# A two-layer cross-attention kernel on one core: plain fp32 scores on four row groups and normalisation by 32x32 block transposes

## The chip, the cores and the metric

One Trainium2 chip, one of its cores. The metric is the device time of one execution of the whole program in microseconds; less is better. Every input starts in HBM and the output ends there. TensorE (PE in the profile) multiplies, PEld is its weight load; DVE is VectorE, ACT is ScalarE, POOL is GpSimd, SP issues the transfers.

## The reference, cut to what matters

The inputs are `x` and `ctx`, each of shape (128, 128, 256): 128 independent tiles of 128 positions. All is fp32. Per tile:

```python
# layer 0: 16 heads of 16, rotary positions, feed-forward width 1024
h = ln(x, ln1);   q, k, v = h@sa_wq, h@sa_wk, h@sa_wv        # plus biases, q scaled, q and k rotated
x = x + softmax(q k^T, causal) v @ sa_wo + sa_bo
h = ln(x, ln2);   q = h@ca_wq;   k, v = ctx@ca_wk, ctx@ca_wv  # plus biases, rotated
x = x + softmax(q k^T) v @ ca_wo + ca_bo
h = ln(x, ln3);   x = x + gelu(h@fc1_w + fc1_b)@fc2_w + fc2_b
# layer 1: fuse, one head of width 256, keys = values = ctx
t = softmax(x ctx^T) ctx
out = tanh([x, t] @ trans_W + trans_b) + x
```

## The kernel before

**Precision.** Most products are done in three fp32r passes, as hi*hi + hi*lo + lo*hi (`split3`, L337 to L342), for which each operand is split: ScalarE or VectorE copies the hi part from PSUM, VectorE subtracts for the lo part (`sub`, L626). PV (L481) and one fuse product (L575) are plain fp32; the trace records each plain fp32 matmul as two.

**The pipeline.** Every engine runs the same hand-written slot (`slot(i, u)`), one new tile per slot, four slots in a loop body. In a slot four tiles are in flight: `a` (first layer norm, self q/k/v, first self scores), `k` = a-1 (second self scores, exponentials, PV, cross keys and values), `m` = a-2 (self output, layer norm 2, the whole cross-attention, layer norm 3) and `f` = a-4 (second feed-forward product and fuse). Every second slot ends in f1, the first feed-forward product for two tiles, followed by gelu (ScalarE), hid_hi (GpSimd) and hid_lo (VectorE). The order of work on each engine is the order in which its `slot` calls the steps; semaphores join the engines, and there is no scheduler. PSUM has eight banks: four are the scores `sc`, and A0, A1, B0, C0 are shared by all the rest.

**Softmax of one chain** (`c` is "s" for self, "c" for cross). The maximum over keys must be known per query before the exponential, but the exponential is taken on transposed scores (keys on partitions), so scores are computed twice:

- q and its low part are put side by side (`qs_hi`, `qs_lo`), k is doubled (`twice`: `kd`, `kcd`), so that one head fills 32 rows, hi and lo. TensorE transposes them (`trq`, `trk`, `trkc`), and ScalarE writes q as a block-diagonal `qt` in four copies of 32 rows (L921, 4 x 577 ns), keys as `skt_hi`/`kct_hi` with VectorE's `skt_lo`/`kct_lo`.
- `scores` (L442): 16 fp32r matmuls of 128x128 with all 128 rows; the self chain first adds a bf16 mask (L424). Each group of four signals.
- `maxima` (L757): four VectorE reductions of 128x512, as each group arrives. `trm` (L455) transposes the 16 maxima, `mdiag` (L762) spreads them.
- `scores_t` (L465, L470): four K=32 matmuls add the negative maximum, eight 128x512 matmuls add the scores. Each pair signals, and `exps` (L947) follows group by group; then `pv` (L481), whose ones columns give the softmax sums.
- Normalisation: ScalarE copies PV out (`osb`), TensorE transposes (`tro`), VectorE takes a reciprocal (L769) and multiplies (L771), TensorE transposes back (`tra`), `at_hi` and `at_lo` split, and `y` multiplies in six fp32r passes. `residual` (L791) adds x and starts the next layer norm, in whose wait for the GpSimd power the cross chain does one self maximum (`meanwhile`).

```python
if X: scores("c", m)      # TensorE, before, around the cross scores
if A: trk(a)
if F: fs(f)
if X: trm("c", m)
if A: trq("s", a)
if X: scores_t("c", m)
if F: trfa(f)
if X: pv("c", m)
if F: fy(f)
```

Of the kernel before, what the change touches and what calls it, by code (L numbers as in the profile page):

```python
# [44 lines left out]
def build(nc, d, out_d):  # L45
    ctx = ExitStack()
    with ctx:
# [48 lines left out]
        kct_hi = sb("kct_hi", [P, G, P], F32R)  # L96
        kct_lo = sb("kct_lo", [P, G, P], F32R)
        skt_hi = sb("skt_hi", [P, G, P], F32R)
        skt_lo = sb("skt_lo", [P, G, P], F32R)
# [27 lines left out]
        qs = {c: sb(f"qs_{c}", [P, H, 2, HD], F32R) for c in "sc"}  # L127

        qt = dict.fromkeys("sc", sb("qt", [P, G, G, P], F32R))
        nm = {c: sb(f"nm_{c}", [P, G, 32], F32R) for c in "sc"}  # L130
        mdiag = dict.fromkeys("sc", sb("mdiag", [P, G, P], F32R))
# [5 lines left out]
        osb = {c: sb(f"osb_{c}", [P, G, P]) for c in "sc"}  # L137
        rinv = {c: sb(f"rinv_{c}", [P, H]) for c in "sc"}
        att = dict.fromkeys("sc", sb("att", [P, H, HD]))
        at_hi = dict.fromkeys("sc", sb("at_hi", [P, KC, P], F32R))  # L140
        at_lo = dict.fromkeys("sc", sb("at_lo", [P, KC, P], F32R))
        mask_f, mask_tf = osb["s"][:, 0, :], osb["s"][:, 1, :]
# [28 lines left out]
        per_chain = ("qs_hi", "qs_lo", "trq", "qt", "sc", "nm", "trm", "mdiag", "sct", "exp", "pv", "osb", "tro",  # L171
                     "rinv", "att", "tra", "at_hi", "at_lo", "y", "x", "xres")
# [959 lines left out]
```

## Time and profile before

| | us |
|---|---|
| median of 3 runs | 5721.84 |
| lowest, highest | 5720.23, 5731.34 |
| span of the profiled execution (first to last instruction) | 5720.3 |
| TensorE busy, 34992 matmuls | 4624.6 |
| TensorE weight loads busy | 3728.5 |
| VectorE busy, 7863 instructions | 3590.9 |
| ScalarE busy, 5121 instructions | 2441.3 |
| GpSimd busy, 1924 instructions | 1298.8 |
| mean granted TensorE clock | 0.920 of full |

The profiled execution's own time is not listed apart from the three runs; its span lies 1.5 us under their median and within their spread. How to read it: an engine's busy time is the sum over all its instructions, so it doesn't tell who waits for whom. A granted clock of 1.00 is 2.4 GHz, 0.50 is 1.2 GHz. A matmul's duration in a row contains its latency; what it costs the queue is the distance of the starts.

### The profile page before, as it was taken

The page shows a single profiled execution, that of the slowest core. Times are in us where ns is not written, and L with a number is a line of the kernel's source. Part 1 is how long each engine was busy: PE and PEld are TensorE (multiplying, and loading weights), DVE is VectorE, ACT ScalarE, POOL GpSimd, SP SyncE. Part 2 cuts the span into 40 slices and gives each one's busy share as a digit, 9 for nine tenths or more (in the row PEclk, how much of TensorE's full clock was granted, in tenths as well). Part 3 has the DMA queues.
Part 4 walks back from the last instruction along what each step waited for, and adds up shares of the span by engine and source line. Part 5 has one row for each costly group of instructions (what it writes and reads, how often), then busy time and mean ns, then how long its engine had stood idle before and what let it go on. Part 6 is the DMA issues. An engine that isn't in the chain of part 4 may idle for free.

```text
span 5720.3 us, 99465 instructions
## 1 busy us (share of the span) xinstructions
PE 4624.6 (81%) x34992; PEld 3728.5 (65%) x34992; DVE 3590.9 (63%) x7863; ACT 2441.3 (43%) x5121; POOL 1298.8 (23%) x1924
## 2 busy tenths in 40 slices
PE   4888888888888888888888888888888888888886
PEld 3666666666666666666666666666666666666665
DVE  4666666666666666666666666666666666666663
ACT  1444444444444444444444444444444444444442
POOL 0222222222222222222222222222222222222221
PEclk7899999999999999999999999999999999999997
DMA  1000000000000000000000000000000000000000
GB/s 55 9 10 10 9 12 10 10 10 12 9 10 12 10 10 10 11 10 10 10 12 9 10 12 10 10 12 10 10 10 12 10 9 11 11 10 10 12 6 5
DMA packets 64812, 63.61 MB, mean 11 GB/s; under 512 B 9648, under 2 KB 64048, under 8 KB 64304
## 3 DMA queue, kind: packets, MB, share of 16 engines
q1 hardware_dynamic: 64304, 56.61, 3.2%
q8 instruction: 346, 5.67, 0.4%
q14 instruction: 162, 1.33, 0.1%
HBM read 39.81 MB, written 16.78 MB: 10 GB/s over the span
## 4 chain that ended last, share of the span: by engine, by line
PE 48%; DVE 25%; issue 16%; POOL 6%; ACT 3%; DVEq 0%; POOLq 0%; ACTq 0%
PE sc L470 10%; DVE nm_c L757 5%; PE B L335 4%; PE A L340 3%; PE A L342 3%; PE A L341 3%; POOL hid_hi L1076 3%; PE C L340 3%; PE C L342 3%; PE C L341 3%; PE B L340 2%; PE A L481 2%; PE sc L465 2%; PE B L481 2%; DVE at_lo L626 2%
## 5 line engine op out<-in xcount | busy, mean ns | idle before, releaser
L947 ACT ACTIVATE pt<-sc 128x512 f32<-128x512 f32 x1024 | 564.1, 599 | 415.0 <-PE sc L470 402.8
L1046 POOL TENSOR_TENSOR rstd<-bmv,eps_t 128x1 f32<-128x1 f32 x384 | 72.7, 189 | 1894.9 <-DVE bmv L674 1894.9
L626 DVE TENSOR_TENSOR hid_lo<-hid,hid_hi 128x512 fp32r<-128x512 f32 x256 | 264.7, 1070 | 353.2 <-POOL hid_hi L1076 353.2
L921 ACT CAST qt<-B 32x512 fp32r<-32x512 f32 x512 | 295.7, 577 | 183.9 <-PE B L335 179.4
L1076 POOL TENSOR_TENSOR hid_hi<-hid,ones_f 128x512 fp32r<-128x512 f32 x256 | 264.7, 1054 | 453.4 <-ACT hid L977 452.7
L757 DVE TENSOR_REDUCE nm_s<-sc 128x4 fp32r<-128x512 f32 x512 | 338.8, 682 | 12.4 <-PE sc L442 5.7
L335 PE MATMUL B<-ident,att 128*128 128x128 f32 x512 | 114.9, 308 | 279.3 <-DVE att L771 279.3
L757 DVE TENSOR_REDUCE nm_c<-sc 128x4 fp32r<-128x512 f32 x512 | 316.2, 674 | 0.0
L340 PE MATMUL C<-w_f_hi,hid_hi 128*128 128x256 f32 x1024 | 302.4, 295 | 3.6 <-POOL hid_hi L1076 3.0
L678 DVE TENSOR_SCALAR xhat<-x,bmv,rstd 128x256 f32<-128x256 f32 x256 | 207.0, 808 | 144.3 <-POOL rstd L1048 144.3
L921 ACT CAST qt<-A 32x512 fp32r<-32x512 f32 x512 | 294.9, 576 | 4.7 <-PE A L335 0.3
L470 PE MATMUL sc<-qt,kct_hi 128*128 128x512 f32 x512 | 294.5, 575 | 0.0
L335 PEld LDWEIGHTS B<-ident,att 128*128 128x128 f32 x512 | 59.2, 147 | 360.1 <-DVE att L771 346.8
L342 PE MATMUL C<-w_f_hi,hid_lo 128*128 128x256 f32 x1024 | 289.3, 282 | 0.0
L341 PE MATMUL C<-w_f_lo,hid_hi 128*128 128x256 f32 x1024 | 289.0, 282 | 0.0
L1082 POOL TENSOR_TENSOR o_out<-fpre,x 128x256 f32<-128x256 f32 x128 | 93.2, 728 | 829.9 <-ACT fpre L995 829.9
L442 PE MATMUL sc<-skt_hi,qt 128*128 128x128 f32 x2048 | 270.7, 286 | 0.0
L887 ACT CAST h3t_hi<-B 128x256 fp32r<-128x256 f32 x128 | 47.6, 372 | 521.2 <-PE B L335 521.2
L470 PE MATMUL sc<-qt,kct_lo 128*128 128x512 f32 x512 | 267.1, 522 | 0.0
L442 PEld LDWEIGHTS sc<-skt_hi,qt 128*128 128x128 f32 x2048 | 252.4, 194 | 19.1 <-issue 0.8
L470 PE MATMUL sc<-qt,skt_hi 128*128 128x512 f32 x512 | 263.2, 514 | 0.0
L442 PEld LDWEIGHTS sc<-kct_hi,qt 128*128 128x128 f32 x2048 | 248.0, 191 | 13.5 <-ACT qt L921 2.7
(249 smaller groups left out, 14323.5 us busy)
## 6 DMA issues: line engine op xcount, KB each, us to landing
rows_in<-in_x SPq DMA_DIRECT2D x128, 128.0 KB, 2.0
rows_in<-in_ctx SPq DMA_DIRECT2D x128, 128.0 KB, 2.1
out<-o_out SPq DMA_DIRECT2D x128, 128.0 KB, 1.7
pt<-in_L_xattn_fc_w SPq DMA_DIRECT2D x1, 1024.0 KB, 4.8
rows_in<-in_L_xattn_fc_w SPq DMA_DIRECT2D x1, 1024.0 KB, 6.8
pt<-in_L_xattn_sa_wq SPq DMA_DIRECT2D x1, 256.0 KB, 8.6
rows_in<-in_L_xattn_sa_wk SPq DMA_DIRECT2D x1, 256.0 KB, 8.6
pt<-in_L_xattn_sa_wv SPq DMA_DIRECT2D x1, 256.0 KB, 2.7
```

The costliest lines, as they stand in the source:

```text
L335: t = pe.transpose(out[:, k * P:(k + 1) * P], src[:, k * P:(k + 1) * P], ident[:, :])
L340: pe.matmul(out, a_hi, b_hi, start=first, stop=False, skip_group_check=True)
L341: pe.matmul(out, a_hi, b_lo, start=False, stop=False, skip_group_check=True)
L342: return pe.matmul(out, a_lo, b_hi, start=False, stop=last, skip_group_check=True)
L442: mm = pe.matmul(sc[:, g, b * P:(b + 1) * P], qt[c][:, g, b, :], kh[:, g, :], start=(b == 0 and c == "c"), stop=(b == G - 1), skip_group_c ...
L470: mm = pe.matmul(sc[:, g, :], kk[:, g, :], qt[c][:, g, :, :].rearrange("p b q -> p (b q)"), start=False, stop=(kk is kl), skip_group_check ...
L481: mm = pe.matmul(bank_of[c]["pv"][32 * b:32 * b + 32, g * P:(g + 1) * P], vaug[c][at[1] % 2][:, G * g + b, :], pt[c][:, g, b, :], start=Tr ...
L626: dve.tensor_tensor(out, a, hi.bitcast(F32), ALU.subtract).then_inc(signal, 1)
L757: dve.tensor_reduce(nm[c][:, g, 0:G], sc[:, g, :].rearrange("p (b k) -> p b k", b=G), AX_X, ALU.max, negate=True).then_inc(sc_[c]["nm"], 1)
L921: w = act.copy(qt[c][part, :, b, :], bank_of[c]["q"][part, :].rearrange("p (g q) -> p g q", q=P))
L947: act.activation(pt[c][:, g, :, :].rearrange("p b q -> p (b q)"), sc[:, g, :], ACT.Exp)\
L1076: pool.tensor_tensor(hid_hi[:, 2 * c:2 * c + 2, :], hid[c % 2][:, :, :], ones_f[:, :].unsqueeze(1).broadcast_to([P, 2, M * P]), ALU.mult). ...
```

## The change

Two parts, in both attention chains.

**Scores.** q and k are no longer split. `rope` writes them with a stride of 32 columns per head into `qkz`, `qcz`, `kcz`: 16 features, a 17th and 15 zeros. After a transpose (plain, the same 4 x 128x128) one head lies in one 32-row group of `qt`/`kt`, copied by ScalarE in one 128x512 copy. `scores` uses the 16 feature rows of each head: 16 plain fp32 matmuls, the four row groups in turn, each group writing its own bank. `maxima` writes the negative maximum straight into the 17th column of q (whose partner in k is one), in two reductions of 128x1024 after all 16 matmuls; `trqm` transposes q again (four transposes), `qtm_` copies it, and `scores_t` is 16 plain fp32 matmuls with all 32 rows. `exps` waits for all of them.

**Normalisation.** VectorE transposes the 32x32 blocks of PV's bank (`ot_`, L722), takes the reciprocal, multiplies in two halves, and transposes the blocks again into `at_t` (L737); `y` is two plain fp32 matmuls against output weights whose rows are loaded in a permuted order (`w_out`, eight small transfers). `ot_("s", k)` stands on VectorE after the cross rope of the same slot, `ot_("c", m)` after `fpre`. osb, tro, tra, at_hi and at_lo are gone.

```diff
@@ TensorE
-                for g in range(G):
-                    for b in range(G):
-                        mm = pe.matmul(sc[:, g, b * P:(b + 1) * P], qt[c][:, g, b, :], kh[:, g, :],
-                                       start=(b == 0 and c == "c"), stop=(b == G - 1), skip_group_check=True)
-                    mm.then_inc(sc_[c]["sc"], 1)
+                    for r in range(G):
+                        rows = slice(32 * r, 32 * r + HD)
+                        mm = pe.matmul(sc[:, r, g * P:(g + 1) * P], qt[c][rows, g, :], kt[c][rows, g, :],
+                                       start=(g == 0 and c == "c"), stop=(g == G - 1), skip_group_check=True)
+                mm.then_inc(sc_[c]["sc"], 1)
...
-                pe.transpose(bank_of[c]["m"][:, 0:P], nm[c][:, :, :].rearrange("p b g -> p (b g)").bitcast(F32),
-                             ident[:, :]).then_inc(sc_[c]["trm"], 1)
+                transposes(bank_of[c]["m"], qz[c].rearrange("p h e -> p (h e)"), G).then_inc(sc_[c]["trqm"], 1)
...
+                pe.wait_ge(sc_[c]["qtm"], n(at))
                 for g in range(G):
-                    pe.matmul(sc[:, g, :], ones_r[32 * g:32 * g + 32, :],
-                              mdiag[c][32 * g:32 * g + 32, :, :].rearrange("p b q -> p (b q)"), start=(c == "c"),
-                              stop=False, skip_group_check=True)
-                for g in range(G):
-                    for kk in (kh, kl):
-                        mm = pe.matmul(sc[:, g, :], kk[:, g, :], qt[c][:, g, :, :].rearrange("p b q -> p (b q)"),
-                                       start=False, stop=(kk is kl), skip_group_check=True)
-                    mm.then_inc(sc_[c]["sct"], 1)
+                    for r in range(G):
+                        rows = slice(32 * r, 32 * r + 32)
+                        mm = pe.matmul(sc[:, r, g * P:(g + 1) * P], kt[c][rows, g, :], qt[c][rows, g, :],
+                                       start=(g == 0 and c == "c"), stop=(g == G - 1), skip_group_check=True)
+                mm.then_inc(sc_[c]["sct"], 1)
...
-                    mm = split3(bank_of[c]["y"][:, 0:E], at_hi[c][:, k, :], at_lo[c][:, k, :], w_hi[w][:, k, :],
-                                w_lo[w][:, k, :], k, k == 0, k == KC - 1)
+                    mm = pe.matmul(bank_of[c]["y"][:, 0:E], at_t[c][:, k, :], w_out[c][:, k, :], start=(k == 0),
+                                   stop=(k == KC - 1))
@@ VectorE
-            def maxima(c, at, groups):
-                for g in groups:
-                    dve.wait_ge(sc_[c]["sc"], G * n(at, 0) + g + 1)
-                    dve.tensor_reduce(nm[c][:, g, 0:G], sc[:, g, :].rearrange("p (b k) -> p b k", b=G),
+            def maxima(c, at, halves):
+                dve.wait_ge(sc_[c]["sc"], n(at))
+                for h in halves:
+                    out = qz[c].rearrange("p (g r) e -> p r g e", r=G)[:, 2 * h:2 * h + 2, :, HD]
+                    dve.tensor_reduce(out, sc[:, 2 * h:2 * h + 2, :].rearrange("p r (g k) -> p r g k", g=G),
                                       AX_X, ALU.max, negate=True).then_inc(sc_[c]["nm"], 1)
...
+            def ot_(c, at):
+                dve.wait_ge(sc_[c]["pv"], n(at))
+                dve.transpose(ot[c][:, :, :, :].rearrange("p r b j -> p (r b j)"), bank_of[c]["pv"][:, :])\
+                    .then_inc(sc_[c]["ot"], 1)
...
+                for k in range(KC):
+                    w = dve.tensor_tensor(att[c][:, k, :, :, :].rearrange("p b s e -> p s b e"),
+                                          ot[c][:, 2 * k:2 * k + 2, :, 0:HD],
...
+                dve.transpose(at_t[c][:, :, :].rearrange("p k q -> p (k q)"),
+                              att[c][:, :, :, :, :].rearrange("p k b s e -> p (k b s e)")).then_inc(sc_[c]["at_t"], 1)
@@ VectorE, slot
-                if X: qs_lo("c", m)
+                if K: ot_("s", k)
...
-                if A: qs_lo("s", a)
-                if X: maxima("c", m, range(G))
-                if A: skt_lo_(a)
-                if X: mdiag_("c", m)
+                if X: maxima("c", m, (0, 1))
...
+                if X: ot_("c", m)
                 if X: normalise("c", m)
-                if X: at_hi_("c", m)
-                if X: at_lo_("c", m)
-                if K: kct_lo_(k)
                 if X: residual("c", m, a if A else None)
+                if X: h3t_lo_(m)
                 if A: maxima("s", a, (1,) if X else (0, 1))
-                if X: h3t_lo_(m)
-                if A: maxima("s", a, (2, 3))
```

On TensorE, from the cross scores of a tile to its output projection. `kd`, `qs_s`, `kcd` are the doubled or split q and k, `nm_c` the maxima. Before:

```order
L442 MATMUL sc<-kct_hi,qt 128x128 x16
L335 MATMUL A<-ident,kd 128x128 x4
L455 MATMUL B<-ident,nm_c 128x128
L335 MATMUL A<-ident,qs_s 128x128 x4
L465 MATMUL sc<-mdiag,ones_r 128x512 x4
L470 MATMUL sc<-qt,kct_hi 128x512
L470 MATMUL sc<-qt,kct_lo 128x512
```

and the changed kernel, where `qkz` and `qcz` are the widened q and k:

```order
L433 MATMUL sc<-kt_c,qt_c 128x128 x16
L333 MATMUL A<-ident,qkz 128x128 x4
L333 MATMUL B<-ident,qcz 128x128 x4
L333 MATMUL A<-ident,qkz 128x128 x4
L454 MATMUL sc<-qt_c,kt_c 128x128 x16
L465 MATMUL B<-pt,vaug_c 32x128 x16
L333 MATMUL A<-ident,kcz 128x128 x4
L478 MATMUL B<-w_out_c,at_t_c 128x256 x2
```

The second score block is 16 matmuls of 128 columns in place of four and eight of 512, one maximum transpose became four, and the transposes between PV and the projection went.

On VectorE, from fpre to the reciprocal of the next slot. Before:

```order
L837 TENSOR_TENSOR fpre<-C,bias_t 128x256
L769 RECIPROCAL rinv_c<-B 128x16
L771 TENSOR_TENSOR att<-B,rinv_c 128x256
L777 CAST at_hi<-B 128x256
L626 TENSOR_TENSOR at_lo<-B,at_hi 128x256
L626 TENSOR_TENSOR kct_lo<-A,kct_hi 128x512
L791 TENSOR_TENSOR x<-B,xres_c 128x256
```

and the changed kernel:

```order
L792 TENSOR_TENSOR fpre<-C,bias_t 128x256
L722 STREAM_TRANSPOSE ot_c<-B 128x512
L727 RECIPROCAL rinv_c<-ot_c 128x16
L730 TENSOR_TENSOR att_c<-ot_c,rinv_c 128x2x4x16 x2
L737 STREAM_TRANSPOSE at_t_c<-att_c 128x256
L746 TENSOR_TENSOR x<-B,xres_c 128x256
L640 BN_STATS bst<-x 128x6
L642 COPY dtick<-eps_t 128x1
L643 BN_AGGR bmv<-bst 128x2
L717 TENSOR_REDUCE qkz<-sc 128x2x4
L647 TENSOR_SCALAR xhat<-x,bmv,rstd 128x256
```

Two block transposes took the place of the two splits, and the self maximum ahead of xhat now covers two banks.

## Rows read from the trace of the kernel before

**Rows 1.** The page: busy time of each engine; the chain that ended last.
```profile
PE 4624.6 (81%) x34992; PEld 3728.5 (65%) x34992; DVE 3590.9 (63%) x7863; ACT 2441.3 (43%) x5121; POOL 1298.8 (23%) x1924
...
PE 48%; DVE 25%; issue 16%; POOL 6%; ACT 3%; DVEq 0%; POOLq 0%; ACTq 0%
```

**Rows 2.** Timeline, VectorE: start us, us, engine line op, out<-in, xcount [idle before].
```profile
2825.51 0.26 DVE L769 RECIPROCAL rinv_s<-B 128x16 f32<-128x16 f32 x1 [1.83 <-issue]
...
2829.79 0.42 DVE L791 TENSOR_TENSOR x<-B,xres_s 128x256 f32<-128x256 f32 x1 [1.29 <-PE B L342]
...
2858.83 0.42 DVE L791 TENSOR_TENSOR x<-B,xres_c 128x256 f32<-128x256 f32 x1
...
2864.30 0.25 DVE L769 RECIPROCAL rinv_s<-B 128x16 f32<-128x16 f32 x1
...
2867.89 0.42 DVE L791 TENSOR_TENSOR x<-B,xres_s 128x256 f32<-128x256 f32 x1 [0.52 <-issue]
...
2896.76 0.42 DVE L791 TENSOR_TENSOR x<-B,xres_c 128x256 f32<-128x256 f32 x1 [0.17 <-PE B L342]
...
2911.81 0.24 DVE L769 RECIPROCAL rinv_s<-B 128x16 f32<-128x16 f32 x1
```

**Rows 3.** Timeline, TensorE: cross scores and fuse product of both slots, first f1.
```profile
2843.05 1.90 PE L442 MATMUL sc<-kct_hi,qt 128*128 128x128 f32 x16
...
2853.65 0.70 PE L575 MATMUL C<-cw,fatt_t 128*128 128x256 f32 x2
...
2881.03 1.90 PE L442 MATMUL sc<-kct_hi,qt 128*128 128x128 f32 x16
...
2891.56 0.70 PE L575 MATMUL C<-cw,fatt_t 128*128 128x256 f32 x2
...
2901.12 0.36 PE L340 MATMUL A<-h3t_hi,w_f_hi 128*128 128x256 f32 x1 [0.97 <-DVE h3t_lo L626]
```

**Rows 4.** Windows of 1 us, TensorE: length, busy (matmuls), granted clock, DMA, GB/s.
```profile
2830.00:2831.00 1.00, 1.00 (x6) 0.50 0.00 0
...
2850.00:2851.00 1.00, 1.00 (x4) 0.50 0.00 0
...
2864.00:2865.00 1.00, 0.56 (x3) 1.00 0.00 0
```

**Rows 5.** Timeline, TensorE: self scores, mask, four transposes.
```profile
2859.26 2.09 PE L442 MATMUL sc<-skt_hi,qt 128*128 128x128 f32 x16
...
2864.60 1.03 PE L424 MATMUL sc<-mask_t_bf,ident_bf 128*128 128x512 bf16 x4
...
2885.58 0.63 PE L335 MATMUL A<-ident,qs_s 128*128 128x128 f32 x4
```

**Rows 6.** Timeline, TensorE, windows to 2873.65, 2873.75 and around 2867.9.
```profile
2873.58 0.32 PE L481 MATMUL A<-pt,vaug_s 128*32 128x128 f32 x4 [0.16 <-DVE tqk L717]
...
2873.58 0.43 PE L481 MATMUL A<-pt,vaug_s 128*32 128x128 f32 x8 [0.16 <-DVE tqk L717]
...
2867.73 0.51 PE L465 MATMUL sc<-mdiag,ones_r 32*128 32x512 f32 x4
```

**Rows 7.** Timeline, VectorE (qs_lo, fpre, the normalised x) and ScalarE (exponentials).
```profile
2882.24 0.51 DVE L626 TENSOR_TENSOR qs_s<-qkf,qs_s 128x256 fp32r<-128x256 f32 x1
...
2893.01 0.42 DVE L837 TENSOR_TENSOR fpre<-C,bias_t 128x256 f32<-128x256 f32 x1 [2.65 <-PE C L342]
...
2860.93 0.81 DVE L678 TENSOR_SCALAR xhat<-x,bmv,rstd 128x256 f32<-128x256 f32 x1 [0.18 <-POOL rstd L1048]
...
2868.95 2.07 ACT L947 ACTIVATE pt<-sc 128x512 f32<-128x512 f32 x4 [2.69 <-PE sc L470]
```

**Rows 8.** Groups of instructions by form: busy us, mean ns | idle before.
```profile
L757 DVE TENSOR_REDUCE nm_c<-sc 128x4 fp32r<-128x512 f32 x512 | 316.2, 674 | 0.0
...
L762 DVE TENSOR_TENSOR mdiag<-B,dmask 128x512 fp32r<-128x512 f32 x128 | 86.2, 673 | 1.0 <-PE B L455 1.0
...
L887 ACT COPY osb_c<-B 128x512 f32<-128x512 f32 x128 | 75.0, 586 | 53.3 <-PE B L481 53.3
```

More of the change, by code:

```diff
@@ L95, in build @@
                 "c": [sb(f"vaug_c{i}", [P, H, 2 * HD]) for i in range(2)]}
[L96 to L99, printed above, removed]
+        kt = {c: sb(f"kt_{c}", [P, G, P]) for c in "sc"}
         tqk = sb("tqk", [P, 2 * E])
@@ L125, in build @@
         o_out = [sb(f"o_out{i}", [P, E]) for i in range(2)]
[L127 to L131, printed above, removed]
+        qt = {c: sb(f"qt_{c}", [P, G, P]) for c in "sc"}
         pt = dict.fromkeys("sc", sb("pt", [P, G, G, P]))
@@ L136, in build @@
         ln_brep = x2b_all[:, 0:3 * KC * P].rearrange("p (l k n) -> p l k n", l=3, k=KC)
-        osb = {c: sb(f"osb_{c}", [P, G, P]) for c in "sc"}
+        ot = {c: sb(f"ot_{c}", [P, G, G, 2 * HD]) for c in "sc"}
         rinv = {c: sb(f"rinv_{c}", [P, H]) for c in "sc"}
[L139 to L142, printed above, removed]
+        att = {c: sb(f"att_{c}", [P, KC, G, 2, HD]) for c in "sc"}
+        at_t = {c: sb(f"at_t_{c}", [P, KC, P]) for c in "sc"}
+        mask_f, mask_tf = [at_t["s"][:, k, :] for k in range(2)]
         xres = {"s": [sb(f"xres_s{i}", [P, E]) for i in range(2)], "c": [sb("xres_c", [P, E])] * 2}
@@ L170, in build @@
         s = {n: sem("s_" + n) for n in names}
-        per_chain = ("qs_hi", "qs_lo", "trq", "qt", "sc", "nm", "trm", "mdiag", "sct", "exp", "pv", "osb", "tro",
-                     "rinv", "att", "tra", "at_hi", "at_lo", "y", "x", "xres")
+        per_chain = ("trq", "qt", "sc", "nm", "trqm", "qtm", "sct", "exp", "pv", "ot",
+                     "rinv", "att", "at_t", "y", "x", "xres")
         sc_ = {c: {n: sem(f"s_{c}_{n}") for n in per_chain} for c in "sc"}
@@ L396, in trq @@
             def trq(c, at):
-                pe.wait_ge(sc_[c]["qs_hi"], n(at))
-                pe.wait_ge(sc_[c]["qs_lo"], n(at))
+                pe.wait_ge(s["qkf" if c == "s" else "qcf"], n(at))
                 if c == "s":
@@ L531, in f1 @@
                 need(pe, s["fpre"], n(f))
-                for q in ("kct_hi", "kct_lo", "tkc", "v_c"):
+                for q in ("kct", "tkc", "v_c"):
                     pe.wait_ge(s[q], n(k))
-                for q in ("skt_hi", "skt_lo"):
-                    pe.wait_ge(s[q], n(a))
+                pe.wait_ge(s["skt"], n(a))
                 for c in range(FC):
```

223 lines of the change are left out of this document (81 added, 142 removed).

## The prediction

> **What bounds the kernel now.** I read the page first: TensorE is busy for 81% of the span and VectorE for 63%, yet the chain that ended last lies on TensorE for only 48% of its length, on VectorE for 25%, and 16% is issue [rows 1]. So no engine is the bound alone. The program is a loop of hand-ordered slots in which TensorE, ScalarE, VectorE and GpSimd pass one tile on to each other, and a saving counts only where one of them waits for it.
>
> So I cut one pair of slots (two tiles) into stages, by the VectorE timeline and the TensorE timeline. Slot A runs from the reciprocal at 2825.51 to the one at 2864.30, slot B, which ends in the first feed-forward product, to 2911.81: 86.30 us for the pair [rows 2]. 64 pairs make 5523 us, the rest of the 5720.3 us span is setup, fill and drain. The stages, A then B [rows 2, 3]:
> - 1, self-attention's normalisation and output projection, reciprocal to x: 4.28 and 3.59.
> - 2, x to the first cross scores: 13.26 and 13.14.
> - 3, cross scores, maximum, second scores, exponentials, PV, to the fuse product L575: 10.60 and 10.53.
> - 4, L575 to cross-attention's x: 5.18 and 5.20.
> - 5, x to the next reciprocal in A, 5.47; to the first f1 product in B, 4.36.
> - 6, only in B: f1, gelu, the hid_hi/hid_lo chain, to the reciprocal, 10.69.
>
> The third view is the granted clock. It stands at 0.50 (1.2 GHz) in A's stage 1 and in stage 3, and at 1.00 around the start of B's stage 1 [rows 4]. In each half-rate stretch TensorE had done little but transposes before.
>
> **The score blocks.** Scores were 16 fp32r matmuls, 2.09 us in the self case [rows 5]; now they are 16 fp32 matmuls of 128 columns on four 32-row groups. The trace has both halves of that. The plain fp32 PV product (four column groups) starts four passes together: x4 last 0.32, x8 last 0.43, so 0.107 us per four passes [rows 6]. Four K=32 matmuls of 512 columns on four row groups last 0.51 together [rows 6], little more than one alone would. 32 passes in eight bursts give 7 x 0.107 + 0.28 = 1.03 us to the last result. Bounds: 1.0, if row groups behave as column groups do; 16 x 0.107 + 0.2 = 1.9, if the two passes of a matmul run one behind the other; 32 x 0.107 = 3.4, if nothing overlaps. I take 1.03, by the nearest row, and use it in both directions of the scores. The Trainium skill, TensorE: Matmul & The Clock Gate, "What overlaps and what doesn't", says matmuls start and end strictly in program order. By that rule the block would be 1.9; the PV rows speak against it, so it stays a rival.
>
> **Stage 3, both slots.** S is the first cross score. VectorE's qs_lo goes, which took 0.51 from S+1.21 [rows 7], just ahead of the maxima; they now start at S+1.25, after the block's end at S+1.06. Four reductions of 674 ns [rows 8] step by 0.60; two of twice the size step by 1.13 and end at S+3.6. Then four transposes, 0.63 [rows 5], in place of one; a copy of 0.59 by ScalarE (its row: 586 ns [rows 8]) in place of mdiag's 0.67 [rows 8]; the block, at S+4.95 instead of S+6.2. Its exponentials now wait for the whole block (S+6.15) and take 2.07 [rows 7] to 2.2, so S+8.3; PV's last quarter adds 0.25. L575 starts at S+8.55, 2.0 earlier than the mean of 10.56. That is at full clock. At half, block, PV tail and L575's products cost 1.85 more. The quiet stretch before the block begins earlier and ends earlier than today's, so I charge half of that: -1.08 per slot.
>
> **Stage 4, both slots.** After L575, fpre (1.45 later, 0.44 with its hand-over [rows 3, 7]) still comes first on VectorE. Then the 512-wide block transpose, which no row shows: I take 0.69, a little over the 512-wide mdiag of 673 ns [rows 8]; the reciprocal 0.29; two half-size multiplies, 0.5; a 256-wide transpose, 0.42, like the 256-wide x [rows 2]. TensorE's two rounds of transposes, osb, at_hi and at_lo go. The plain fp32 projection has four passes of 256 columns; two such in L575 last 0.70 [rows 3], so four last 1.13 against 0.75. Sum 5.03, -0.17. The bounds of the wide transpose: 0.67 (the mdiag and reduction rows), and twice 0.69, since nothing here excludes half rate.
>
> **Stage 5.** The mask (four matmuls, 0.68 before the next starts) is unchanged, scores end at x+1.5, and the first maximum now needs all of them: x+1.55 instead of x+1.2, and lasts 1.13 instead of 0.6. The normalisation waits for it, at x+2.72 instead of x+2.10, but then runs beside no GpSimd work (0.42, like x [rows 2], instead of 0.81 [rows 7]). Sum: +0.15 in A, +0.2 in B.
>
> **Stage 1.** In A, at half clock: reciprocal, multiplies, transpose 1.2, projection 1.95, x at 3.3: -1.0. In B, TensorE first has four transposes where one was and then the mask, so the projection starts at 1.4 and x comes at 2.5 at full clock, 4.6 at half. Between scores (end 2861.35) and mask (2864.60) there are 3.25 us without matmuls today, at 1.00 [rows 4, 5]; that stretch grows to 4.6, nearer to the long ones that end at 0.50. I take 4.0: +0.4.
>
> **Stages 2 and 6.** Stage 2's products and their VectorE queue are untouched; qs_hi, twice and the four-part qt copies (ScalarE), and qs_lo, skt_lo, kct_lo (VectorE) go, all beside TensorE's f2 to kvc products, so nothing is gained; the moved 0.69 us transpose of the self chain is hidden there too, and would cost its own 0.69 if those products were shorter. Exponentials that start later push x2t_hi back: +0.2 and +0.25. f1 may begin at half clock after the longer quiet: +0.3 for stage 6. Setup loses two weight splits and gains eight transfers, within 3 us, at nothing.
>
> Sum: A -1.0 +0.2 -1.08 -0.17 +0.15 = -1.90; B +0.4 +0.25 -1.08 -0.17 +0.2 +0.3 = -0.10. That is -2.0 us per pair, -128 us, a span of 5592 from 5720.3. The shown median, 5721.84, stands 1.5 above that span, so 5594.
>
> **The rivals.**
> - The clock. TensorE sheds over a tenth of its work, and each quiet stretch is longer. If the half-rate stretches also cover the mask and scores of stage 5 (+1.7 each) and all of stage 3 (+0.92 each), the pair is +5.2, +335 us: 5930; half of that, which I find likelier, is 5760. It decides from +2.0 us per pair on, that is, when one of the two stage 5s and one stage 3 run at 1.2 GHz. For it: the rows at 0.50 today. Against: the long dense run of stage 2 lifts the clock each time. Chance 0.2.
> - Passes in order: +0.75 (maxima late), +0.85 (second block), +0.85 (stage 5), +0.15 elsewhere, 2.6 per slot, 5.2 per pair: 5927. For it the page's rule, against it the PV rows. Chance 0.12.
> - Block transposes at half rate: +1.1 in stage 4, +0.4 in stage 1 per slot, 3.0 per pair: 5786. Chance 0.06.
> - The clock stays up: stage 3 at full (-1.85 per pair), B's stage 1 at 2.5 (-1.5), stages 2 and 6 without their charges (-0.6): -3.95, -253 us: 5341. Against: rows 4. Chance 0.1.
> - Gains and losses cancel (the change surely does what it says: the order rows show the new queues). Within 0.2%, about what a measurement of this kernel can tell from no change: 5710 to 5733. Chance 0.05.
>
> **How the numbers follow.** The forecast, 5594, has what is left, 0.47, and spans about 5500 to 5700. Faster: forecast 0.47, clock up 0.1, and a tenth or two of the clock rival's low end: 0.61. Same 0.06. Slower 0.33. The range must hold eight in ten: it reaches down over half of the clock-up case to 5440 and up over the half-rate transposes and most of the clock rival to 5860; passes in order stays outside.
>
> **What would show it.** Each score block in the new trace: 1.0 us at full clock, eight starts of four passes 0.107 apart (1.9 would mean passes in order). The 512-wide transpose near 0.69. The pair near 84.3 us; stage 3 near 9.5 and near 8.6 where the clock is 1.00; stage 5 slightly longer. Mean granted clock a little under 0.92; under 0.85 the clock rival holds. The forecast is wrong if stage 3 isn't a microsecond shorter, or if stage 5 or 1 grows by more than that.

## The result, and the profile after

The changed kernel takes 5982.66 us (median of 4, 5971.28 to 6004.51) against 5721.53 us: ratio 1.0454, 95% interval 1.0437 to 1.0472. It is slower by 261 us; 5594 us was forecast, and the range ended at 5860. The profiled execution spans 5969.5 us with a mean granted clock of 0.846, where the kernel before spans 5720.3 us at 0.920.

The page, beside [rows 1]: busy time of the engines, the granted clock in 40 slices, the chain that ended last.

```profile
PE 4462.0 (75%) x42928; PEld 3482.7 (58%) x42928; DVE 3205.1 (54%) x6966; ACT 1706.6 (29%) x3713; POOL 1330.2 (22%) x1924
...
PEclk9888888888888888888898888888888888888887
...
issue 43%; PE 20%; DVE 18%; POOL 11%; ACT 6%; DMA 0%; SPq 0%; POOLq 0%; DVEq 0%; ACTq 0%
```

Every engine but GpSimd does less work, as intended: VectorE 386 us less, ScalarE 735 us less, TensorE 163 us less. TensorE's saving is that small because much of what is left runs at half rate: in experiment x4, where the clock is higher, TensorE is busy for 4403 us, 479 of them with added idle matmuls. The kernel is longer all the same, so the time went into waits and into slower work. "issue", which grew from 16% to 43% of the chain, does not tell slow from fast here: it reads 44% in x4 and 41% in x12, the fastest kernel below.

The VectorE timeline over a pair of slots, beside [rows 2]:

```profile
2846.34 0.24 DVE L727 RECIPROCAL rinv_s<-ot_s 128x16 f32<-128x16 f32 x1
...
2849.46 0.42 DVE L746 TENSOR_TENSOR x<-B,xres_s 128x256 f32<-128x256 f32 x1 [1.23 <-issue]
...
2878.46 0.42 DVE L746 TENSOR_TENSOR x<-B,xres_c 128x256 f32<-128x256 f32 x1 [1.28 <-PE B L478]
...
2884.43 0.24 DVE L727 RECIPROCAL rinv_s<-ot_s 128x16 f32<-128x16 f32 x1
...
2889.19 0.42 DVE L746 TENSOR_TENSOR x<-B,xres_s 128x256 f32<-128x256 f32 x1 [2.87 <-issue]
...
2919.01 0.42 DVE L746 TENSOR_TENSOR x<-B,xres_c 128x256 f32<-128x256 f32 x1 [2.22 <-PE B L478]
...
2936.36 0.25 DVE L727 RECIPROCAL rinv_s<-ot_s 128x16 f32<-128x16 f32 x1
```

The TensorE timeline of the same pair, beside [rows 3, 5]:

```profile
2864.10 1.17 PE L433 MATMUL sc<-kt_c,qt_c 16*128 16x128 f32 x32
2869.09 1.17 PE L454 MATMUL sc<-qt_c,kt_c 32*128 32x128 f32 x32 [0.24 <-ACT qt_c L836]
...
2877.24 1.13 PE L478 MATMUL B<-w_out_c,at_t_c 128*128 128x256 f32 x4 [2.53 <-DVE at_t_c L737]
2878.20 1.03 PE L415 MATMUL sc<-mask_bf,ident_bf 128*128 128x512 bf16 x4
...
2912.47 0.70 PE L547 MATMUL C<-cw,fatt_t 128*128 128x256 f32 x2
...
2916.84 2.08 PE L478 MATMUL B<-w_out_c,at_t_c 128*128 128x256 f32 x4 [2.53 <-DVE at_t_c L737]
2918.71 1.60 PE L415 MATMUL sc<-mask_bf,ident_bf 128*128 128x512 bf16 x4
2920.24 1.17 PE L433 MATMUL sc<-kt_s,qt_s 16*128 16x128 f32 x32
```

The score blocks last 1.17 us (1.03 forecast). The same projection lasts 1.13 us in slot A and 2.08 in slot B, and both times TensorE had sat idle for 2.53 us before it. The granted clock in 1 us windows of slot B, beside [rows 4], shows why:

```profile
2915.00:2916.00 1.00, 0.00 (x0) 1.00 0.00 0
2916.00:2917.00 1.00, 0.15 (x1) 0.72 0.00 0
2917.00:2918.00 1.00, 1.00 (x3) 0.50 0.38 131
...
2920.00:2921.00 1.00, 1.00 (x26) 1.00 0.00 0
...
2922.00:2923.00 1.00, 0.00 (x0) 1.00 0.00 0
2923.00:2924.00 1.00, 0.55 (x2) 0.64 0.00 0
...
2929.00:2930.00 1.00, 1.00 (x6) 0.50 0.07 16
2930.00:2931.00 1.00, 1.00 (x10) 0.95 0.00 0
```

TensorE idles at 1.00 while VectorE normalises, the clock drops to 0.50 (1.2 GHz) just as projection and mask begin, is back at 1.00 (2.4 GHz) for the scores, idles through the layernorm and drops again for the first 5 us of f1. What stands behind the quiet stretch pays for it, on the path. The same stage of this one trace says it without any comparison of kernels. Here is B4 in three pairs that follow each other (columns as in [rows 4]):

```profile
2734.83:2741.37 6.54, 4.02 (x21) 0.81 0.14 46
2823.92:2829.52 5.60, 3.08 (x22) 1.00 0.08 26
2912.47:2919.01 6.54, 4.01 (x21) 0.80 0.12 42
```

The stage lasts 5.60 us at a clock of 1.00 and 6.54 at 0.8.

The new VectorE work, by form (busy us, mean ns | idle before). The transposes are means of like instructions; the 546 ns of att_c are not, see x7:

```profile
L730 DVE TENSOR_TENSOR att_c<-ot_c,rinv_c 128x128 f32<-128x128 f32 x256 | 129.3, 546 | 4.4
...
L722 DVE STREAM_TRANSPOSE ot_c<-B 128x512 f32<-128x512 f32 x128 | 90.3, 706 | 6.7 <-PE B L465 6.7
...
L737 DVE STREAM_TRANSPOSE at_t_c<-att_c 128x256 f32<-128x256 f32 x128 | 57.0, 445 | 4.4
```

One pair is a sample, since the clock falls in other places in the next. So here are the stages as means in us over some 55 pairs of each trace, cut by the same rows (first and last start of each stage); the forecast's own charge stands beside them, and the last column is experiment x4, below.

| stage | before | forecast | after | after − before | x4 − before |
|---|---|---|---|---|---|
| A1 | 4.00 | −1.0 | 3.34 | −0.66 | −1.12 |
| A2 | 13.83 | +0.2 | 14.68 | +0.85 | +0.79 |
| A3 | 10.27 | −1.08 | 9.13 | −1.14 | −1.51 |
| A4 | 5.19 | −0.17 | 6.29 | +1.10 | +0.41 |
| A5 | 5.46 | +0.15 | 6.58 | +1.12 | +0.51 |
| B1 | 3.62 | +0.4 | 4.71 | +1.09 | −0.92 |
| B2 | 13.10 | +0.25 | 14.14 | +1.04 | +1.07 |
| B3 | 10.38 | −1.08 | 8.86 | −1.52 | −1.62 |
| B4 | 5.20 | −0.17 | 6.16 | +0.96 | +0.40 |
| B5 | 4.36 | +0.2 | 5.59 | +1.23 | +0.59 |
| B6 | 11.67 | +0.3 | 11.82 | +0.15 | −0.98 |
| pair | 87.08 | −2.0 | 91.31 | +4.23 | −2.37 |

What was to get faster did. What was charged at next to nothing, the stages that hold projection, mask and self scores, grew by more than a microsecond each. 64 pairs of +4.23 make +271 us, the whole difference of the spans (249) and a little more.

One row of the table, B6, hides two effects. In the kernel before it alternates (a loop body holds two pairs), and not by the clock: in experiment x6, below, both lengths stand at 1.00.

```profile
2812.92:2825.51 12.59, 8.05 (x61) 0.98 0.01 3
2901.12:2911.81 10.69, 8.06 (x61) 1.00 0.01 2
```

In the longer one VectorE stands idle for 1.83 us ahead of the reciprocal and waits for nothing that the profile shows [rows 2]. The pair that the forecast was read from ends in the short one. The changed kernel doesn't have this: in x4, at a clock of 1.00, B6 is 10.69 us in every pair. So the change wins 1 us per pair there that nobody forecast, and the clock takes it back (11.82 against 10.69). What causes the wait no run shows; x1, with the new scores alone, hasn't got it, and x2 has.

### The profile page after: what moved, and what is told of

It is laid out like the page before. It is cut to its first block, busy times and chain, and to the rows that moved or that the text cites. A ratio compares the mean times of both kernels' runs of the same rounds, so it can differ in the third digit from the quotient of the medians.

```text
span 5969.5 us, 110993 instructions
## 1 busy us (share of the span) xinstructions
PE 4462.0 (75%) x42928; PEld 3482.7 (58%) x42928; DVE 3205.1 (54%) x6966; ACT 1706.6 (29%) x3713; POOL 1330.2 (22%) x1924
## 4 chain that ended last, share of the span: by engine, by line
issue 43%; PE 20%; DVE 18%; POOL 11%; ACT 6%; DMA 0%; SPq 0%; POOLq 0%; DVEq 0%; ACTq 0%
PE B L478 4%; POOL hid_hi L996 4%; ACT pt L882 4%; PE sc L454 3%; POOL qkf L957 3%; DVE qkz L717 3%; DVE qcz L717 3%; PE B L333 2%; PE sc L415 2%; DVE att_c L730 2%; PE A L333 2%; POOL kcf L957 2%; POOL xres_c L981 2%; PE sc L433 2%; DVE ot_c L722 1%
## 5 line engine op out<-in xcount | busy, mean ns | idle before, releaser
L836 ACT COPY qt_c<-B 128x512 f32<-128x512 f32 x256 | 150.3, 587 | 1140.2 <-PE B L333 1140.2
L478 PE MATMUL B<-w_out_c,at_t_c 128*128 128x256 f32 x512 | 224.2, 583 | 320.4 <-DVE at_t_c L737 320.4
L717 DVE TENSOR_REDUCE qkz<-sc 128x8 f32<-128x1024 f32 x256 | 312.4, 1221 | 170.2 <-PE sc L433 170.2
L333 PE MATMUL A<-ident,qkz 128*128 128x128 f32 x1536 | 283.0, 315 | 99.8 <-DVE qkz L717 89.2
L478 PE MATMUL B<-w_out_s,at_t_s 128*128 128x256 f32 x512 | 231.0, 600 | 154.4 <-DVE at_t_s L737 154.4
L717 DVE TENSOR_REDUCE qcz<-sc 128x8 f32<-128x1024 f32 x256 | 301.6, 1221 | 7.2 <-PE sc L433 1.3
L333 PE MATMUL B<-ident,qcz 128*128 128x128 f32 x1024 | 165.0, 284 | 168.4 <-DVE qcz L717 164.6
L465 PE MATMUL B<-pt,vaug_c 128*32 128x128 f32 x4096 | 217.0, 291 | 91.2 <-ACT pt L882 73.8
L478 PEld LDWEIGHTS B<-w_out_s,at_t_s 128*128 128x128 f32 x512 | 148.0, 302 | 229.6 <-issue 192.2
L333 PEld LDWEIGHTS A<-ident,qkz 128*128 128x128 f32 x1536 | 196.7, 159 | 144.0 <-DVE qkz L717 114.0
```

The source lines that it names most:

```text
L333: t = pe.transpose(out[:, k * P:(k + 1) * P], src[:, k * P:(k + 1) * P], ident[:, :])
L465: mm = pe.matmul(bank_of[c]["pv"][32 * g:32 * g + 32, r * P:(r + 1) * P], vaug[c][at[1] % 2][:, G * g + r, :], pt[c][:, r, g, :], start=Tr ...
L478: mm = pe.matmul(bank_of[c]["y"][:, 0:E], at_t[c][:, k, :], w_out[c][:, k, :], start=(k == 0), stop=(k == KC - 1))
L717: dve.tensor_reduce(out, sc[:, 2 * h:2 * h + 2, :].rearrange("p r (g k) -> p r g k", g=G), AX_X, ALU.max, negate=True).then_inc(sc_[c]["nm ...
L836: act.copy(out, src).then_inc(signal, 1)
```

## The experiments

The theory: TensorE lost work between its bursts, the quiet stretches end at 1.2 GHz more often, and the work behind them pays. Its first rival: VectorE's chain is longer and collides with GpSimd, and TensorE only waits for it. Its second: one of the two parts of the change alone is the loss. Times below are medians against runs of the kernel before on the same chip.

**x1 and x2: the parts apart.** x1 keeps the old normalisation (osb, two rounds of transposes, hi/lo split, fp32r projection) and has the new scores; x2 keeps the old scores and has the new normalisation, with w_out's rows permuted to the old order of heads. The main edit of each, x1 against the changed kernel and x2 against the one before:

```
x1:  +                if X: tro("c", m)
     +                if X: tra("c", m)
                      if K: trkc(k)
                      if X: y("c", m)
x2:  -                if X: tro("c", m)
     -                if X: tra("c", m)
                      if K: trkc(k)
                      if X: y("c", m)
```

Expected of x1: 

> The kernel before with the score part of the change alone; the old normalisation (evacuation, two rounds of transposes, fp32r projection) stays. Two theories on the 261 us that the change cost. Clock theory: TensorE lost work in its quiet stretches, these end at 1.2 GHz more often, and mask, scores, projection and transposes behind them run at half rate. Then the old rounds of transposes, still there in front of each projection, keep part of the rate up: stages 3 as in the changed kernel, stage 4 near the old 5.2 us, total 5650 to 5800. VectorE theory: the loss is in the longer VectorE chain (block transposes, a product of 1.02 us beside GpSimd's copy, maxima that wait for the whole block). Then this kernel keeps the late maxima but not the dear normalisation: 5700 to 5800 with stage 5 as long as in the changed kernel and the granted clock unchanged at full speed in it.

Expected of x2: 

> The kernel before with the normalisation part alone (32x32 block transposes, plain fp32 projections); scores as they were. Clock theory: TensorE has nothing between the fuse product and the projection, so projection, mask and scores of stages 4 and 5 run at half rate: stages 4 and 5 about 1 us longer each, 5800 to 5950, mean clock 0.85 to 0.88. VectorE theory: stage 4 longer by about 1 us at an unchanged clock, stage 5 as before: about 5790.

x1: 5806.96 us, ratio 1.0152 (1.0128 to 1.0175), clock 0.893, just above both expected ranges; stage 4 stays near the old one (5.21 and 5.43 us), as the clock theory had it, and the largest loss is B1, 5.42 us at a clock of 0.65. x2: 5713.78 us, ratio 0.9978 (0.9968 to 0.9988), clock 0.910. For x2 both theories were wrong: its stage 4 stayed at 5.19 and 5.15 us, and its cross projection kept the rate (mean 435 ns per matmul; 583 in the changed kernel, 408 in x4 below). B1 fell from 3.62 to 2.88. The two effects multiply to 1.013 where both together give 1.045: some 3% of the time, about two thirds of the loss, appears only when both parts are there, so the second rival falls. The new scores alone cost 83 us. In x2 the products att_c last 290 ns in the mean, not 546; I come back to that in x7.

**x3: the mask earlier.** The causal mask of the self scores needs nothing of its slot but free banks. Here it is issued while TensorE would idle before the projection.

```
-                if c == "s":
-                    causal_mask(mask_bf)
...
+                if A: early_mask(a)
                 if X: y("c", m)
                 if A: scores("s", a)
```

Expected: 

> The changed kernel with the causal mask of the self scores issued ahead of the cross projection, in TensorE's quiet stretch, in place of behind it. Clock theory: the mask (0.68 us at full rate, 1.4 at half) leaves the path of stage 5, and ahead of the projection it also lifts the clock for it: -1.5 to -2.5 us per slot pair plus, 5780 to 5880, mean clock above 0.846. VectorE theory: stage 5 waits for VectorE (the next layernorm step and the maxima), so at most 0.7 us per slot: 5890 or more, the clock unchanged.

5607.21 us, ratio 0.9796 (0.9779 to 0.9813), clock 0.888. That is 375 us under the changed kernel for a move of four matmuls that adds and removes nothing, more than any theory gave. The mask is 0.68 us on the path at full rate: for 128 tiles 87 us. The rest goes with the clock: stage 4, from which nothing was taken away, fell from 6.29 and 6.16 us to 5.60 in both slots, which is its length at a clock of 1.00 in the changed kernel too.

**x4: filler.** Matmuls whose results are never read, put where TensorE is idle:

```
+            def warm(bank, count):
+                for _ in range(count):
+                    pe.matmul(bank.rearrange("p (g k) -> p g k", g=G), ident_bf[:, :],
+                              mask_bf[:, :].unsqueeze(1).broadcast_to([P, G, P]), start=True, stop=True,
+                              skip_group_check=True)
...
+                if A and X: pe.wait_ge(s["skt"], n(a))
+                if A and X: warm(A1[:, :], 3)
                 if X: trqm("c", m)
...
+                if A and X: warm(sc[:, 0, :], 6)
                 if X: y("c", m)
                 if A: scores("s", a)
+                if F: pe.wait_ge(s["fpre"], n(f))
+                if F: warm(C0[:, :], 6)
```

Expected: 

> The changed kernel plus idle work for TensorE whose results nobody reads: three 512-column bf16 matmuls ahead of the cross transposes with the maximum, six ahead of the cross projection, six behind the self scores. Nothing is taken away. Clock theory: the granted clock rises from 0.846 to 0.93 or more and the kernel gets faster, to 5650 to 5850, although TensorE has more to do. VectorE theory: no gain, 5980 to 6080, since TensorE was not late.

5551.41 us, ratio 0.9695 (0.9678 to 0.9713), clock 0.952. TensorE is given more to do and the kernel is 431 us faster than without. Where slot B of the changed kernel fell to 0.50, the windows now read:

```profile
2883.00:2884.00 1.00, 0.00 (x0) 1.00 0.00 0
2884.00:2885.00 1.00, 0.85 (x4) 1.00 0.38 131
2885.00:2886.00 1.00, 1.00 (x6) 1.00 0.39 67
```

and the timeline of TensorE:

```profile
2881.46 1.46 PE L421 MATMUL sc<-mask_bf,ident_bf 128*128 128x512 bf16 x6
2884.15 1.13 PE L484 MATMUL B<-w_out_c,at_t_c 128*128 128x256 f32 x4 [1.23 <-DVE at_t_c L748]
2885.12 1.03 PE L415 MATMUL sc<-mask_bf,ident_bf 128*128 128x512 bf16 x4
2886.07 1.17 PE L439 MATMUL sc<-kt_s,qt_s 16*128 16x128 f32 x32
```

Projection 1.13 for 2.08, mask 1.03 for 1.60, and f1 begins at full rate (B6 10.69 us, from 11.82). The VectorE theory, which expected nothing from this run, falls as the main cause; what is left of it is stage 4, at 5.60 us in place of the 5.19 of before, and half a microsecond of stage 5. The Trainium skill, TensorE: Matmul & The Clock Gate, "HAM oscillation — how this bites in real kernels", describes the same picture for waits on transfers (bursts of matmuls, a wait, half rate for the next burst) and advises, for that kernel, to restructure the loop so that TensorE stays busy; these runs show the same picture with waits on VectorE in place of transfers (2.53 us idle, then 2.08 us for a projection that lasts 1.13 at full rate).

**x8: one filler.** Only the six matmuls ahead of the cross projection.

Expected: 

> The changed kernel with one of the three fillers alone, the six matmuls ahead of the cross projection. Clock theory: this place holds the rate for projection, mask and self scores (stages 4 and 5, 2.2 us per pair lost there beside the 0.9 of the longer VectorE work), while the stretches behind stay: 5700 to 5830, clock about 0.89. If the rate after each quiet stretch is lost on its own, the gain is only the projection's 0.8 us per slot: 5870 to 5890.

5715.09 us, ratio 0.9982 (0.9971 to 0.9993), clock 0.890. Stages 4 and 5 read 5.65, 5.98 in A and 5.70, 4.97 in B, nearly as in x4, while B1 (4.54) and B6 (11.55) stay near the changed kernel's. Time and clock are as the clock theory expected. This one place wins 4.0 us per pair (91.31 to 87.29) of the 6.6 that x4 wins: 2.3 in stages 4 and 5, most of the rest in A1 and B2 (2.87 and 13.46 us). The stretches ahead of B1 and B6 have to be filled apart.

**x5: mask and filler together.** x3 and x4, with three fillers before the early mask, and six more where x4 still fell:

```
                 if K: scores_t("s", k)
+                if K and X: warm(A1[:, :], 6)
                 if X: trx2(m)
```

Expected: 

> The changed kernel with both: the causal mask ahead of the cross projection (with three filler matmuls ahead of it), three fillers ahead of the cross transposes, six behind the self scores, and six more behind the second self scores, where the run with filler still showed half rate: there TensorE sat idle for 1.95 us before the x2 transposes and the cross query projection behind them ran at 0.21 us per matmul instead of 0.12. Clock theory: against that run's 5551 us the mask gives 0.5 us per slot of stage 5 and the fillers 0.6 to 0.9 us per slot of stage 2, together 2.2 to 2.8 us per pair: 5370 to 5420, clock 0.96 or more. If stage 2 is longer for another reason (the exponentials that start late), it stays at 14.2 us and the time at 5500 or more.

5459.5 us, ratio 0.9535 (0.9516 to 0.9553), clock 0.961. Stage B2 falls from 14.17 to 13.20 us (before: 13.10). The longer stage 2 of B was thus the clock too, and x4's own pairs say the same:

```profile
1330.77:1345.23 14.46, 12.51 (x127) 0.88 0.00 1
1414.82:1427.99 13.17, 11.07 (x127) 1.00 0.01 1
```

Which edit did it is open: in x3, with the early mask and no filler, B2 is already 13.31 us. A2 keeps half a microsecond of its growth (14.33 against 13.83). The time misses the expected 5370 to 5420, since stage 1 grew, from 2.88 to 3.39 and from 2.70 to 3.35. Its TensorE timeline shows the next place, at the head of the slot behind a feed-forward group:

```profile
2847.11 0.43 PE L333 MATMUL A<-ident,rows_in 128*128 128x128 f32 x2 [1.85 <-ACT hid L919]
...
2848.39 1.91 PE L415 MATMUL sc<-mask_t_bf,ident_bf 128*128 128x512 bf16 x4
2851.62 2.07 PE L486 MATMUL B<-w_out_s,at_t_s 128*128 128x256 f32 x4 [1.32 <-DVE at_t_s L752]
```

**x7: GpSimd's sum later.** x4, with o_out's sum behind x2b's on GpSimd's queue.

```
-                if F: fout_(f)
                 if X: rstd_(2, m)
                 if X: x2b_(m)
+                if F: fout_(f)
```

Expected: 

> The changed kernel with the same filler as x4, and GpSimd's sum o_out, which runs beside VectorE's att_c products, put behind the x2b sum on GpSimd's queue. If the products last 1.02 us instead of 0.49 because of that sum, they go back to 0.49 and stage 4 from 5.60 to about 5.1: 0.5 us per slot, 5490 to 5520. If the length has another reason, nothing changes within 0.3%. What speaks against a full gain: the sum then runs beside the layernorm of stage 5 or the hid_hi chain.

5498.14 us, ratio 0.9604 (0.9588 to 0.962), clock 0.936. The products' row, by form:

```profile
L741 DVE TENSOR_TENSOR att_c<-ot_c,rinv_c 128x128 f32<-128x128 f32 x256 | 63.2, 289 | 4.5
```

289 ns in place of 546, and stage 4 falls from 5.60 to 5.08 and 5.07 us, as expected. The 546 was the mean of two unlike products. In the trace of the changed kernel:

```profile
L730 DVE TENSOR_TENSOR att_c<-ot_c,rinv_c x256: 277/293/816, 133.4 to 5922.5; 128x128 f32<-128x128 f32 x128
...
2915.29 1.02 DVE L730 TENSOR_TENSOR att_c<-ot_c,rinv_c 128x128 f32<-128x128 f32 x2
2915.33 0.83 POOL L1002 TENSOR_TENSOR o_out<-fpre,x 128x256 f32<-128x256 f32 x1 [4.31 <-ACT fpre L922]
```

(The first line gives shortest, median and longest, in ns.) The first product starts ahead of GpSimd's sum and lasts 0.29 us; the second starts while the sum runs, lasts 0.81 us and ends 0.15 us after it. So this is not two instructions that share a rate: the second product stands until the sum is through. Both read and write SBUF only. In A1 some clock went back (2.88 to 3.30 us).

**x11: mask and sum, no filler.** Expected: 

> The changed kernel with the early mask (x3) and GpSimd's o_out sum behind x2b (x7), no filler: nothing in it is there for the clock alone. By x7's 0.5 us per slot: 5607 - 60 = 5545, if the shorter stage 4 has no other effect; 5520 to 5580.

5641.75 us, ratio 0.9854 (0.9833 to 0.9876), clock 0.873: a miss. The edit that won 53 us with filler loses 35 without (5607 to 5642; the two intervals lie apart). Stage 4 did fall, from 5.60 to 5.12, but A3 rose from 8.76 to 9.08 and B6 from 11.15 to 11.72. In both the clock is lower (0.93 for 1.00 in A3). Making VectorE faster here went with a lower clock of TensorE, and I did not find out by which stretch.

**x6: filler in the kernel before, first try.** Three matmuls ahead of trm("c"), two ahead of tro("c"), six behind the self scores.

Expected: 

> The kernel before, whole, with filler in its own quiet stretches (three ahead of the transposed maxima, two ahead of the cross output's transposes, six behind the self scores). It asks what the half-rate stretches cost the old kernel, so that the two can be compared at the same clock. If the score and normalisation path is worth what the prediction's sum said, this stays 100 us or more above the changed kernel with filler (5551), at 5640 or more. If the old kernel gains as much from filler as it has half-rate time on the path (1.3 us in stage 1 of A, 0.9 in each stage 3: 3 us per pair), it comes to 5530, and the change is worth nothing at an equal clock.

6033.53 us, ratio 1.0544 (1.0526 to 1.0561), clock 0.921: my edit, not the clock. The filler's bank is read by skt_lo, which VectorE does behind the maxima, so TensorE waited for it with the transposed maxima queued behind:

```profile
2840.78 0.94 PE L430 MATMUL A<-mask_bf,ident_bf 128*128 128x512 bf16 x3 [1.87 <-DVE skt_lo L638]
```

Stage 3 rose to 11.93 and 11.41 us. Filler has to fit its gap and wait for nothing.

**x9: filler in the kernel before, second try.**

```
+                if X: warm(B0[:, :], 3)
                 if X: trm("c", m)
...
+                if K and u % 2 == 0: warm(sc[:, 0, :], 7)
                 if K: causal_mask(mask_t_bf)
```

Expected: 

> The kernel before with filler that waits for nothing and fits its gaps: three 512-column matmuls in the 1.20 us before the transposed cross maxima, and seven, only in the slot behind a feed-forward group, ahead of the transposed mask, where TensorE then sits idle for 2.70 us. The first try (x6) had stood on the path, behind a ScalarE/VectorE pair of copies, and read 6034. If the clock is what the old kernel loses in stage 3 (0.9 us each) and in stage 1 of A (1.2 us), this reads 5540 to 5600, and the change is worth nothing at an equal clock. If the half-rate stretches of the old kernel stay (they come from something else) or filler costs what it gives: 5700 or more.

5642.51 us, ratio 0.9866 (0.9826 to 0.9906), clock 0.957, between the two cases. Both stages 3 fall to 9.74 us (10.27 and 10.38) and A1 to 3.46, while B1 and B6 rise to 3.91 and 12.15, both at 0.89. At nearly the same mean clock the changed kernel (x4, 0.952) is 91 us faster, 0.9695/0.9866 = 0.983. But an equal mean is not an equal clock in each stage: x4 has B6 at 1.00 and its two stages 2 at 0.87 and 0.91, x9 the other way round.

A better estimate takes each stage only from the pairs in which its clock reads 1.00 (medians, for each of the two pairs of a loop body), from x9 for the old kernel and from x4 for the new, both with filler. These stages add up to 84.5 and 82.6 us per pair. So the change is worth about 1.9 us per pair, some 119 us, at full clock; as it stands, the clock takes this back and 261 us more. By stage: stages 3 −0.98 each, B1 −0.98, B6 −0.97, A1 −0.55; against it stages 4 +0.40 each, A5 +0.51, B5 +0.58, A2 +0.63, B2 +0.07.

**x10: the early mask in the kernel before.** Between its two rounds of transposes.

Expected: 

> The kernel before with the causal mask of the self scores ahead of its cross projection (between its two rounds of transposes, where TensorE idles for 0.81 us). The mask's 0.68 us goes off stage 5 in both slots: 1.4 us per pair, 5630 to 5650, if stage 5 is bound by mask and scores. It tells whether the 375 us that the same move gave the changed kernel (5983 to 5607) is the move's own worth or the clock's: clock theory says the old kernel gains at most 100 us from it.

5896.74 us, ratio 1.0297 (1.028 to 1.0315), clock 0.881: a miss. The move that won 375 us in one kernel costs 168 in the other. Stage 5 does not change (5.53 and 4.38 us from 5.46 and 4.36: it was VectorE's, not TensorE's), so the scores only end earlier and TensorE idles for longer before the x3 transposes, 1.31 us where it was 0.44. Then, in slot B:

```profile
2852.00:2853.00 1.00, 0.63 (x4) 1.00 0.00 0
2853.00:2854.00 1.00, 0.78 (x3) 0.73 0.00 0
2854.00:2855.00 1.00, 1.00 (x3) 0.50 0.00 0
```

B1 goes from 3.62 to 5.08 us. In the kernel before the same place is at 1.00 [rows 4]: one moved mask was enough to bring the old kernel's clock down there.

**x12: all of it.** x5, x7's sum, and two more fillers:

```
+                if K and u % 2 == 0: pe.wait_ge(sc_["s"]["nm"], 2 * n(k))
+                if K and u % 2 == 0: warm(sc[:, 0, :], 6)
                 if K: trc(k)
...
                 if X: trx3(m)
+                if F and u % 2 == 0: warm(C0[:, :], 4)
```

Expected: 

> x5 (early mask and filler, 5459) with GpSimd's sum moved, and two more fillers: six matmuls at the head of the slot behind a feed-forward group (TensorE idle for 1.85 us there in x5, after which transposes, mask, projection and scores ran at 1.2 GHz), and four behind the x3 transposes of the other slot. Clock theory: stage 1 falls to 2.8 and 2.7 us (3.39 and 3.35 in x5), stage 4 to 5.1: 2.2 us per pair, 5300 to 5350, clock 0.97 or more. If stage 1 stays, the place is wrong: 5390 to 5410.

5312.21 us, ratio 0.9268 (0.9252 to 0.9285), clock 0.975: faster than the kernel before by 7.3%, than the changed one by 670 us. Stages: A 3.01, 14.09, 8.76, 5.07, 5.39; B 2.62, 13.19, 8.76, 5.07, 4.36, 10.69; the pair 81.01. It lies in the expected range. It carries 23 idle matmuls per tile; without any, but with the same two moves, x11 stands at 5642.

## Why the prediction was wrong

- **The score blocks: right.** 1.17 us, against 1.03 forecast and 1.9 by passes in order. The 32 passes start four at a time, 7 ns apart, and the eight bursts are 0.112 us apart (0.107 forecast) but for the first step of 0.21, which makes up most of the difference. So the rival of passes in order is out. The order of starts and ends that the Trainium skill's "What overlaps and what doesn't" gives is not refuted by it: in this block's records starts and ends do come in order. What failed is the 1.9 us that the prediction derived from that rule, by letting the two passes of a matmul hold up the next row group.
- **Stage 3: right.** −1.14 and −1.52 us for −1.08 each. At full clock it is 8.76 us (x4), where the sum had 8.55. It ran at 0.94 and 0.98 in the mean, higher than before (0.90 and 0.84), where the sum had charged half of the price of half rate and the clock rival all of it.
- **Block transposes: right.** 706 ns for 690, 445 for 420; the half-rate rival is out.
- **Stage 4: wrong.** −0.17 was charged, +1.10 and +0.96 measured. 0.5 is the second att_c product, which stands until GpSimd's sum is through (x7: 0.81 to 0.28 us), a wait that the sum did not have. The rest is the projection at half rate (x4: 6.29 to 5.60). Without both it is 5.08, 0.1 below the old one, near the 5.03 of the sum, whose terms as listed add up to 4.92 only. I had taken TensorE's transposes away from in front of the projection and still priced it at 1.13.
- **Stage 5: wrong.** +1.12 and +1.23 for +0.15 and +0.2. x4 splits it: 0.6 is the clock. Of the other 0.5 the sum had a third: the new scores begin 0.95 us after the mask (x4's timeline), not 0.68, and the first maximum 1.94 us after x, not 1.55. VectorE's timeline in slot A of x4:

```profile
2847.94 0.42 DVE L757 TENSOR_TENSOR x<-B,xres_c 128x256 f32<-128x256 f32 x1 [1.28 <-PE B L484]
...
2849.88 1.23 DVE L728 TENSOR_REDUCE qkz<-sc 128x8 f32<-128x1024 f32 x1 [0.78 <-PE sc L439]
```

  It waits 0.78 us for the scores, so mask and scores had come onto the path, and moving the mask takes that back (x3: A5 5.53).
- **Stage 1 of B: wrong in size.** +0.4 was a mean between full and half clock; it came out at half (+1.09). At full clock it is 2.62 us, near the 2.5 named for full rate. In A −1.0 was charged at half clock and −0.66 measured, at 0.74.
- **Stage 2: wrong.** +0.2 and +0.25 for +0.85 and +1.04. The old second scores filled TensorE's time until the x2 transposes (idle for 0.55 us in B); the new ones leave it idle there for 1.9 us, and in most pairs the products behind ran at half, 0.41 us each where 0.28 is full rate. Timeline of x4:

```profile
2821.84 0.44 PE L333 MATMUL B<-ident,xhat 128*128 128x128 f32 x2 [1.95 <-DVE xhat L658]
...
2824.58 0.41 PE L339 MATMUL B<-w_cq_lo,x2t_hi 128*128 128x256 f32 x1
```

  B's microsecond is the clock (13.17 us wherever it reads 1.00); of A's growth 0.6 us stays at full clock, and no run takes that apart.
- **Stage 6: the right number for the wrong reason.** +0.15 for +0.3, but as −0.98, the wait in every second pair that went, and +1.13 for f1 at half rate.
- **The step that failed** is thus the clock's charge. The sum had counted as half rate only what was half rate before, plus 0.4 us in B1 and 0.3 for f1; the runs show half rate behind the new quiet stretches in stages 1, 2, 4, 5 and 6, 6.6 us per pair by x4 (91.31 to 84.71), where the whole forecast was −2.0. The rival "the clock" had mechanism and direction, and its marker (mean clock under 0.85) came true at 0.846; of its places stage 5 held and stage 3 did not, and its full price, 5930, was still too low. It got 0.2, because stage 2's dense work "lifts the clock each time". It does, but the quiet stretches behind it drop it again within the slot. The forecast's own signs of being wrong came true too: stages 5 and B1 grew by more than a microsecond. A second, smaller step failed at full clock as well: stages 4 and 5 had no term for the wait behind GpSimd's sum and too small a one for mask and scores.
- **Luck.** At full clock the change is worth some 119 us, near the 128 of the sum. That is chance in part, two misses of opposite sign: stages 4 and 5 cost 1.9 us per pair at full clock where the sum had nothing, and B1 and B6 win 1.9 us where it charged 0.7.

## What to carry to other kernels

In a pipeline in which the engines wait for each other at every step, removing TensorE work from between its bursts can cost more than it saves: read the granted clock in 1 us windows around each wait on the path, and price what stands behind every stretch that grows at half rate. When a change of this kind reads slower, run it once with idle matmuls that wait for nothing, placed in the gaps; that separates what the change is worth from what the clock takes. Useful work that can be moved into the gap (here the mask) may then fill it for good, but has to be tried: it won in one kernel and lost in the other. Before a version is thrown away, compare it stage by stage where the clock reads 1.00; an equal mean clock can hide unequal stages.

## What was not expected of the hardware

- One edit has opposite signs in two kernels: the early mask gives −375 us at a clock that rises from 0.846 to 0.888 (x3), and +168 us at one that falls from 0.920 to 0.881 (x10).
- Effects do not add: 1.015 and 0.998 alone, 1.045 together. And a shorter VectorE chain can cost time: x11 against x3, +35 us at a clock of 0.873 for 0.888.
- Two idle stretches of the same length, 2.53 us ahead of the same projection, ended once at full rate (1.13 us) and once at half (2.08 us).
- A VectorE product of 128x128 (SBUF to SBUF) that starts while GpSimd's 128x256 sum runs ends only 0.15 us after it, 0.81 us long in place of 0.28; one that starts just ahead of the sum takes its usual 0.29.
